# Moving one eighth of a depthwise convolution from VectorE to TensorE, with five smaller edits and a new order

## The reference

```python
# layer 0
h = silu(bn(einsum(ln(x), w_exp)))             # 96 -> 576 channels
h = silu(bn(depthwise_3x3(h, w_dw)))           # 576 channels, 9 taps each
s = sigmoid(silu(h.mean((2, 3)) @ w_se1.T + b1) @ w_se2.T + b2)   # one gate per channel
x = x + ln(x) + bn(einsum(h * s, w_proj))      # 576 -> 96
x = x + q_linear(relu(q_linear(q(ln(x)), W1)), W2)                # 96 -> 384 -> 96
# layer 1
y = gelu(gn(w1 @ ln(x) + b1))                  # 96 -> 96
z = sum of four gelu(w2 @ shifted(y) + b2)     # shifts by one row and/or column, by thirds of channels
x = x + w3 @ gn(z) + b3
x = x + q_linear(relu(q_linear(q(ln(x)), W1)), W2)
```

## Time and profile before

| what | value |
|---|---|
| runs | 6387.1, 6403.85, 6413.86 us, median 6403.85 us |
| profiled execution | 6384.17 us, span 6382.4 us |
| busy: PE, DVE, ACT, POOL | 5312.2 (83%), 5441.0 (85%), 4393.5 (69%), 509.3 (8%) us |
| mean granted TensorE clock | 0.962 of full |
| chain that ended last, by engine | PE 45%, DVE 31%, ACT 14%, issue 7%, DMA 2%, SPq 2% |

### The profile page before, as it was taken

One profiled execution on the slowest core, in us unless ns is written; L12 is line 12 of the kernel. 1 busy time (PEld: TensorE's weight loads), 2 busy tenths in 40 slices (PEclk: granted clock), 3 DMA queues, 4 the chain that ended last, 5 costly groups with the idle time before them and its releaser, 6 DMA issues.

```text
span 6382.4 us, 158185 instructions
## 1 busy us (share of the span) xinstructions
PE 5312.2 (83%) x63744; PEld 2261.2 (35%) x63744; DVE 5441.0 (85%) x8976; ACT 4393.5 (69%) x7671; POOL 509.3 (8%) x366
## 2 busy tenths in 40 slices
PE   2688888888888888888888888888888888888885
PEld 0233333333333333333333333333333333333332
DVE  5888898888898888998888888888988888988874
ACT  1467776767777767776767776667776767767665
POOL 1100000000000000000000000000000000000000
PEclk9899999999999999999999999999999999999997
DMA  1233333333333333333333333333423333423322
GB/s 47 55 92 94 98 85 85 89 95 94 98 85 89 86 94 95 96 89 85 87 94 94 97 82 85 92 90 94 100 76 93 92 92 93 101 72 94 94 66 68
DMA packets 395662, 559.44 MB, mean 88 GB/s; under 512 B 71490, under 2 KB 391427, under 8 KB 391771
## 3 DMA queue, kind: packets, MB, share of 16 engines
q1 hardware_dynamic: 394940, 549.32, 34.1%
HBM read 233.66 MB, written 78.68 MB: 49 GB/s over the span
## 4 chain that ended last, share of the span: by engine, by line
PE 45%; DVE 31%; ACT 14%; issue 7%; DMA 2%; SPq 2%; ACTq 0%; POOL 0%; DVEq 0%
PE bank L525 24%; DVE conv L877 19%; PE b_banks L525 6%; PE bank L578 5%; ACT hidden L800 3%; ACT hidden L793 3%; PE bank L565 2%; PE b_banks L681 2%; DVE hidden L933 1%; PE sums_b L532 1%; DVE bn_stats L948 1%; ACT mid L733 1%; ACT ffn_out L807 1%; DVE conv L874 1%; PE sums_a L532 1%
## 5 line engine op out<-in xcount | busy, mean ns | idle before, releaser
L877 DVE SCALAR_TENSOR_TENSOR conv<-mid,w_dw,conv 128x1568 f32<-128x1568 f32 x1536 | 2914.1, 1897 | 20.5
L525 PE MATMUL bank<-x,centering 128*32 128x392 f32 x6144 | 839.1, 498 | 143.1 <-DVE b_q L1108 103.3
L525 PE MATMUL bank<-conv,w_proj_gated 128*32 128x392 f32 x7680 | 895.6, 496 | 0.0
L681 PE MATMUL b_banks<-shifted,w_combo 128*32 128x392 f32 x6144 | 621.5, 528 | 314.4 <-DMA shifted<-g 162.6
L525 PE MATMUL bank<-xc_a,w_exp 128*32 128x392 f32 x6144 | 791.7, 514 | 93.6 <-DVE xc_a L860 40.5
L793 ACT ACTIVATE hidden<-b_banks 128x1176 f16<-128x1176 f32 x512 | 595.0, 1162 | 213.8 <-PE b_banks L525 213.5
L800 ACT ACTIVATE hidden<-hidden 128x1176 fp8e5<-128x1176 f16 x512 | 614.7, 1201 | 37.8 <-DVE hidden L933 37.8
L733 ACT ACTIVATE mid<-bank 128x392 f32<-128x392 f32 x768 | 384.5, 510 | 371.4 <-PE bank L525 366.2
L1020 POOL TENSOR_TENSOR x<-x,xc_a 96x392 f32<-96x392 f32 x256 | 489.8, 1914 | 1859.1 <-DVE xc_a L860 1859.1
L525 PE MATMUL b_banks<-xn,w_q 128*32 128x392 fp8e5 x6144 | 542.3, 339 | 58.7 <-ACT hidden L793 45.6
L578 PE MATMUL bank<-phases,w_toeplitz 128*32 128x392 f32 x4608 | 469.1, 523 | 29.5 <-ACT conv L751 14.6
(11 more groups left out here) (170 smaller groups left out, 7688.2 us busy)
## 6 DMA issues: line engine op xcount, KB each, us to landing
phases_on<-phases SPq DMA_DIRECT2D x768, 101.5 KB, 2.4
shifted<-g SPq DMA_DIRECT2D x512, 149.6 KB, 2.7
r_b<-rstd_row_b SPq DMA_DIRECT2D x512, 147.0 KB, 3.0
shifted<-g SPq DMA_DIRECT2D x256, 199.5 KB, 3.0
x<-in_x SPq DMA_DIRECT2D x32, 1176.0 KB, 7.4
r_a<-rstd_row_a SPq DMA_DIRECT2D x256, 147.0 KB, 3.2
x_plus_norm<-x SPq DMA_DIRECT2D x256, 147.0 KB, 2.7
r_a<-x_plus_norm SPq DMA_DIRECT2D x256, 147.0 KB, 2.3
```

Source lines behind the costliest of these rows:

```text
L525: last = mm(o[j:j + QUAD, :], weights[:, j:j + QUAD], x, start=start, stop=stop)
L681: last = mm(rows(PB[32 * u:32 * u + 32, m, 0:TW]), WC[:, u // 2, 32 * m:32 * m + 32], SH[t % 2][:, u, :].rearrange("p (h w) -> p h w", w=G ...
L877: v.scalar_tensor_tensor(out=acc, in0=src, scalar=WDW[:, k, j:j + 1], in1=acc, op0=ALU.mult, op1=ALU.add).then_inc(sem["convolved"], 1)
```

## The change

It has six parts.

1. **Units.** UNITS goes from 3 to 4. The new unit 0 does chunk 0's channels in the first half of the image, by TensorE; VectorE's nine taps for it, its `silu2`, and three of chunk 0's eight `expand` tiles go. ACC0 has two buffers for three, and the semaphore `convolved` becomes two, one for each half.
2. **Sums of squares.** All four matmuls of `var_rows` write to column tile 3 (partitions 96 to 127), 32 rows of sums. The row goes to DRAM in one DMA for four.
3. **Seeds.** The first guess takes one integer operation for two.
4. **gn.** 1/sqrt of the one number per channel is a power on GpSimd (`root`) in place of nine operations on VectorE. The step `gn` is cut in four (`gn`, `gn_spread`, `gn_var`, `gn_affine`), so that others can stand between them.
5. **Centred 1x1 weights.** In the setup w1 is multiplied by the centring matrix. `conv1`'s input is then the uncentred x times 1/sqrt, and `center 1` on ScalarE only squares: the copy into `g` goes.
6. **Order.** All of TIMES is new. It has another set of numbers in each row, such as this one:

```diff
-        "dw 0 0": (6757, 6980, 7225, 7290, 7722, 7845, 8072, 8160, 8459),
-        "dw 0 1": (9078, 9332, 9824, 9885, 10022, 10080, 10294, 10599, 10639),
+        "dw 0 1": (9013, 9328, 9439, 9524, 9935, 10185, 10536, 10719, 11063),
```

The core of the rest:

```diff
-UNITS, SLOTS = 3, 4
-NGR = (MID - NDV * 128) // 32
+UNITS, SLOTS = 4, 4
+NGL = (MID - NDV * 128) // 32
+NGR = NGL + SLOTS
...
-    def conv(k, h, parity):
-
-        return ACC[k][:, h * HALF * WW:(h + 1) * HALF * WW] if k else ACC0[2 if h else parity][:, :]
+    def conv(k, h):
+
+        return ACC[k][:, h * HALF * WW:(h + 1) * HALF * WW] if k else ACC0[h][:, :]
...
-        return (p, u) if u < 2 else (SLOTS + p % 2, p // 2)
+        return (NGL + p, 0) if u == 0 else (p, u - 1) if u < UNITS - 1 else (SLOTS + p % 2, p // 2)
...
-        nc.vector.tensor_scalar(y.bitcast(i32), v.bitcast(i32), 1, None, ALU.logical_shift_right)\
-            .then_inc(sem[s], 1)
-        nc.vector.wait_ge(sem[s], at(base + 2))
-        nc.vector.tensor_scalar(y.bitcast(i32), y.bitcast(i32), -1.0, RSQRT_SEED, ALU.mult, ALU.add)\
+        nc.vector.tensor_scalar(y.bitcast(i32), v.bitcast(i32), -0.5, RSQRT_SEED, ALU.mult, ALU.add)\
             .then_inc(sem[s], 1)
...
-            slices = dram.rearrange("(t j c) -> j t c", t=NT, j=VT)
-            for j in range(VT):
-                sp.dma_start(slices[j, :, :], Y[bufs][QUAD * j:QUAD * j + NT, :])\
-                    .then_inc(sem[f"rstd_stored_{th}"], 16)
+            sp.dma_start(dram.rearrange("(r c) -> r c", r=VR), Y[bufs]).then_inc(sem[f"rstd_stored_{th}"], 16)
...
-            row = ROW[:, NT - 1 - t:NT - 1 - t + QUAD]
             for j in range(VT):
-                last = mm(VPS[th][QUAD * j:QUAD * j + QUAD, :], row, sq[:, j * VW:(j + 1) * VW],
-                          start=(t == 0), stop=(t == NT - 1))
+                r = VT * t + j
+                last = mm(VPS[th], ROW[:, VR - 1 - r:VR - 1 - r + QUAD], sq[:, j * VW:(j + 1) * VW],
+                          start=(r == 0), stop=(r == VR - 1))
...
-                    if L == 1:
-                        act.wait_ge(sem["normed_b"], at(NT * (3 * b - 1) + t + 1))
                     act.wait_ge(sem["varsummed_b"], at(NT * q + t - 1))
                     act.wait_ge(sem["centered_b"], at(NT * q + t + 1))
-                    center_out(o, tile(XCB, t), SQB[t % 2][0:C, :], "squared_b")
+                    if L == 1:
+                        f(SQB[t % 2][0:C, :], o, ACT.Square).then_inc(sem["squared_b"], 1)
+                    else:
+                        center_out(o, tile(XCB, t), SQB[t % 2][0:C, :], "squared_b")
...
                 if L == 1:
-                    v.tensor_tensor(tile(XCB, t), tile(XCB, t), RB[t % 2][:, :], ALU.mult)\
+                    v.tensor_tensor(tile(XCB, t), tile(XB, t), RB[t % 2][:, :], ALU.mult)\
                         .then_inc(sem["normed_b"], 1)
...
-                    if k == 0:
-                        dve.wait_ge(sem["projected"], at(NT * (m if h else m - 1)))
-                    v.tensor_scalar(acc, src, WDW[:, k, j:j + 1], None, ALU.mult).then_inc(sem["convolved"], 1)
+                    if k <= 1:
+                        dve.wait_ge(sem["projected"], at(NT * m))
+                    v.tensor_scalar(acc, src, WDW[:, k, j:j + 1], None, ALU.mult).then_inc(convolved, 1)
...
+            elif name == "root":
+                pool.wait_ge(sem["gn_vector"], at(GN_V * (2 * b + arg[0] + 1)))
+                g.tensor_tensor(col(GY), col(GV), HALVED[:, :], ALU.pow).then_inc(sem["gn_rstd"], 1)
```

More of the change, by code:

```diff
@@ L130 @@
 LEAD = {
-    1: ("load_x", "center_a", "var_a", "rstd_a", "fetch_a", "norm_a", "save_s", "expand 0", "expand 1", "dw 0 0", "dw 0 1"),
+    1: ("load_x", "center_a", "var_a", "rstd_a", "fetch_a", "norm_a", "save_s", "expand 0", "expand 1", "dw 0 1"),
     0: ("expand 2", "dw 1 0", "dw 1 1", "dw 2 0", "dw 2 1", "silu2 0", "silu2 1", "silu2 2", "texp 0", "texp 1",
-        "texp 2", "tconv 0", "tconv 1", "tconv 2", "se1", "se2", "se3", "fetch_s", "proj", "x1", "center 0", "var 0",
+        "texp 2", "texp 3", "tconv 0", "tconv 1", "tconv 2", "tconv 3", "se1", "se2", "se3", "fetch_s", "proj", "x1", "center 0", "var 0",
         "rstd 0"),
@@ L203, in program @@
     SQA = [sb(f"sq_a{n}", [128, TW], fp32) for n in range(2)]
-    RA = [sb(f"r_a{n}", [C, TW], fp32) for n in range(2)]
+    RAFULL = [sb(f"r_a{n}", [128, TW], fp32) for n in range(2)]
+    RA = [buf[0:C, :] for buf in RAFULL]
     XN8 = [sb(f"xn8_{n}", [128, TW], fp8) for n in range(2)]
@@ L334, in g_pads, with col @@
         return G[:, 2 * GP:2 * GP + HH * GP].rearrange("p (h w) -> p h w", w=GP)[:, :, 0:1]
+    def col(c):
+        return GN[:, c:c + 1]
     def rows(ap):
@@ L603, in tensor_steps @@
                 for k in range(NCH):
-                    columns(o, WPS[:, k, :], tile(conv(k, t // NTH, parity), t % NTH, 128), start=(k == 0), stop=False)
+                    columns(o, WPS[:, k, :], tile(conv(k, t // NTH), t % NTH, 128), start=(k == 0), stop=False)
                 columns(o, WPS[:, NCH + t // NTH, :], tile(ACC4, t % NTH, 128), start=False, stop=True)\
```

196 lines of the change are left out of this document (109 added, 87 removed), and 100 rows, old and new, of the table TIMES.

## The result

| what | before | after |
|---|---|---|
| runs, median | 6404.7 us | 6433.0 us (10 runs, 6418.1 to 6447.5) |
| ratio, 95% interval | 1 | 1.0046 (1.0030 to 1.0063) |
| profiled execution, its span | 6384.2, 6382.4 us | 6425.1, 6423.3 us |
| mean granted clock of TensorE | 0.962 | 0.948 |

The account below looks back on a forecast made before the run. A turn was taken as TensorE's work in stage 1 plus VectorE's in stages 2 and 3; -4.5 us times 31 (-140), fill -14, drain -6 gave 6224 us profiled, 6244 us for the runs; range 6100 to 6385 us.

Parts of the forecast that it names:

- The taps: Nine VectorE taps go, 16.1 us per image, but from between gate and last x1, where VectorE has 12 us to spare.
- the fill: Time before the first `se1`: the nine taps there are on the path, -16 us, less 2 us for longer setup.
- Stage 1: Gate to last x1, TensorE full: -0.7 us per turn, from -1.5 of its work and 0.8 for `gn 1`.
- The power on GpSimd: 1/sqrt in `gn`: 0.3 us, with two hand-overs 0.6, bounds 0.1 and 2.56, for nine operations taking 1.7 us.
- Stage 2: Last x1 to end of feed-forwards: -0.5 us per turn, bounds -2 and +2, TensorE's busy time rising to 53.4 us.
- Stage 3: End of feed-forwards to next gate: -3.3 us per turn, bounds 0 and -7, by a shorter, earlier-starting chain after `gn 0`.
- B: Rival: sums of squares in one column tile hold up TensorE's array, +11.8 us per turn, 6750 us; chance 0.08.
- C: Rival: VectorE reaches its own demand in stages 2 and 3, -10.5 us per turn, 6058 us; chance 0.15.
- A: Rival: nothing comes of it, relief where VectorE had time, TensorE binding stage 2; -0.2 us per turn, 6378 us; chance 0.12.
- The side "slower": The outcome of a slower whole kernel, given 0.08, made up of B with a mild form of it.

Follow-up runs that it names:

- b2_fewtaps: Kernel before, with eight of the nine taps of chunk 0's first half cut to one row of 56 positions each: 6382.4 us, ratio 0.9978.
- e10: e5 with the sums of squares back in four column tiles and four DMAs for the row vector: 6294.1 us.
- e13: e5 with five sets of four matmuls that nobody reads added ahead of `se1`, in all images but the first: 6182.2 us.
- e2: Changed kernel with the power of `gn 1` behind two more additions in GpSimd's queue: 6365.9 us.
- e1: Changed kernel with the next image's load ahead of the store of the second rstd row in SyncE's queue: 6270.5 us.
- b3: Kernel before, with all sums of squares of a tile in column tile 3 and one DMA for four: 6434.4 us, ratio 1.0056.
- e5: Changed kernel with the next image's load ahead of the rstd store and the power of `gn 1` behind two more additions: 6235.2 us.

## Why the prediction was wrong

- **The taps.** Right: hidden in stage 1, worth only the fill (b2_fewtaps: 12 us, taken as 16). The rest of the fill, 7 us, was lost again; to what was not tried.
- **Stage 1.** Right in most of its terms: VectorE 20 us busy, TensorE full, part 2 of the change 1.4 us (forecast 1.9) by e10. Measured from `se1` the stage is longer all the same, 58.6 us for 57.2. The missing term is the clock: 8.6 us at the low level for 2.9, and the forecast priced TensorE's work as if at one clock. At e13's 0.36 us for each us these 5.8 us are worth about 2.1 us, an estimate; without them the stage would be 0.7 us shorter than in before, which is about the forecast. Why after has more of the low level is only in part shown: TensorE's idle time in the 5 us ahead of `se1` is 1.8 us for 1.2, but e2 has 5.7 us at the low level with the same idle time ahead of it.
- **The power on GpSimd.** 0.547 us a piece (of 64), forecast 0.3; with hand-overs, from the end of VectorE's operation (3306.85) to the start of the next (3307.52), 0.67 for 0.6. The bounds held. What I left out: what it lets go behind it stretches VectorE's three small operations by 2.4 us. I looked at whether the additions would be in time, not at what they run beside.
- **Stage 2.** -2.3 us for -0.5, just beyond the bound of -2. TensorE is busy 50.4 us of 52.9 in the window, not 53.4, so it binds less than was feared. The forecast added 6.6 us to its busy time there, and 3.6 came.
- **Stage 3.** This is the step that failed: "its start comes 1.1 us earlier by the power. So the end comes up to 3.7 us earlier, and I take -3.3", with 0 as the worst. Means over the 21 turns, from the last add: norm 1 begins at 13.0 us in before, 15.2 in after, 11.7 in e1; `gn 0` ends at 35.5, 37.1 and 32.6. From there to the end of the last fold (of `gelus`) it is 44.2, 41.2 and 40.3 us. So the chain did get shorter by 3.0 us, as forecast (2.6 of table loads). But its start came 1.6 us later for 1.1 earlier, by the load that now stood in the queue ahead of `r_b`. I had read the order on VectorE and TensorE, and of SyncE's queue only the number of issues.
- The same step failed at its other end: "So the end comes up to 3.7 us earlier" takes it that `se1` follows the fold. In after it comes 3.4 us behind it, 44.5 us behind `gn 0` for 44.1 in before, so that the shorter chain gained nothing. What `se1` waits for is the SiLU of the last taps:

```profile
3297.45 1.84 DVE L898 SCALAR_TENSOR_TENSOR conv<-mid,w_dw,conv 128x1568 f32<-128x1568 f32 x1
```

```profile
3299.42 1.28 ACT L780 ACT_TABLE_LOAD   x1
3300.71 1.70 ACT L780 ACTIVATE conv<-conv,bn_affine 128x1568 f32<-128x1568 f32 x1
```

  From `gn 0` to the end of the last tap VectorE is busy 40.6 of 41.1 us in after, 35.9 of 36.6 in before (18 multiply-adds there for 16), and from that end to `se1` it is 3.5 us for 7.5. VectorE's work and the SiLU behind it had taken over the end of the turn. The forecast saw both ends fall together, and took -3.3 nonetheless.
- **The rivals.** B, sums that hold up the array: refuted by b3, 1.2 us a turn and not 11.8, and by e10, where they are a gain. The rule of the Trainium skill behind it ("TensorE: Matmul & The Clock Gate", section "Packing small matmuls — row/col tiling", that matmuls start and end strictly in order) does not agree with the starts in the earlier trace rows, nor with these prices. C had VectorE bound by its own work in stage 3, which is so behind `gn 0`, but took a gain from it. A came nearest to the time, 6378 us, by another mechanism than the one measured. The side "slower" came by queue order, which no rival of mine named.
- With two numbers of the order changed (e5) the distance of `se1` is (6015.3 - 232.5) / 31 = 186.5 us and the time 6235 us. These are the forecast's own numbers, 186.5 and 6244, but that is luck in part: stage 2 gives more (-2.2 for -0.5), stage 3 less (-2.5 for -3.3, from the last add to `se1`), and `se1` to last x1 -0.3 for -0.7. In e1 stage 3 is down by just the 3.3 us of the forecast, but 2.9 of them come from an earlier end of `gn 0` (forecast 1.1) and 0.4 from what follows.
